# DLRM tower kernel: x goes to SBUF first and is copied from there to PSUM, and ScalarE forms the second layer's sums over d

## The chip, the core and the metric

The kernel runs on one core of one Trainium2 chip. The metric is the device time of one execution in microseconds (us), as a median over runs. A core has TensorE (PE, matrix products), VectorE (DVE), ScalarE (ACT), GpSimd (POOL), SyncE (SP, which only issues transfers here), a buffer SBUF and an accumulator memory PSUM. Every engine works through its own list of instructions in order, and the lists meet at semaphores.

## What is computed

`embeddings` is gathered from 32 tables, (2048, 32 fields, 16 numbers d). Three layers of products of fields follow, each gives 64 rows per sample, and then a small perceptron.

```
x0 = embeddings                       # (b, m, d) = (2048, 32, 16)
xk = x0
for W in (W0, W1, W2):                # (32, h, 64)
    xk = relu(einsum('bmd,bhd,mhk->bkd', x0, xk, W))
    outs.append(sum(xk, axis=2))      # the sum over d
z = concatenate(outs, axis=1)
h = concatenate([z, dense_ctx], axis=1)
h = relu(h @ W_top1 + b_top1); h = relu(h @ W_top2 + b_top2)
y = h @ W_top3
```

All numbers are float32.

## The kernel before

The batch is cut into 32 steps of 64 samples; a step has 1024 columns (64 samples x 16 d). The product of a field with a row of xk is made on the vector engines for 128 (field, row) pairs at a time, a chunk (128 x 1024), and TensorE sums the chunks with the weights: `contract` (L808) issues four matmul records of 512 columns for one chunk. The first layer (`layer0`) takes 5 chunks `p_l0`, the second (`layer1`) and third (`layer2`) take 16 each.

**VectorE** makes 15 of the 16 chunks of each of these two layers (`products`, L706), into a ring of ten chunks, `p_dve`. It multiplies the gathered fields, `spread` (SBUF), with the layer's input x. x lies in PSUM in two forms: `xa`, the plain one, for chunks 0 to 6, and `xb`, with the two halves of 32 rows swapped, for chunks 8 to 15. There is one `xa` and one `xb` for both layers. GpSimd makes chunk 7 (`p_pool`) from a third copy of x, `x_s`, which lies in SBUF, and four of the five first-layer chunks; it also issues the gathers. ScalarE makes the fifth by a square.

**A turn** s of the main loop goes in this order on VectorE: second layer of step s (7 chunks from `xa`, 8 from `xb`), then third layer of step s-1 (again 7 from `xa`, 8 from `xb`). Between them it makes sums over d (`sums`, L728, 128x512 to 128x32): ahead of the first `xb` part those of the second layer of step s-2 (from `out_l[:, 1]`), behind it those of the third layer of step s-2. Sums of the first layer are made by ScalarE from s = 4 on (`sums_0`, L493): one ACTIVATE over 16 columns with an accumulated output for each sample, 32 in a step, in two halves.

**TensorE** in a turn: the 16 chunks of the second layer (accumulator `acc1`, two of them in turns), from s = 4 on with one part of the perceptron behind chunk 5 (`mlp_pair`, parts 0 to 3 in four turns, part 2 twice the size of parts 0 and 1); then third-layer chunks 0 to 3 (`acc2`), the five chunks of the *first* layer of step s+1 (`layer0`, accumulator `acc0`), and third-layer chunks 4 to 15.

**ScalarE** evicts: `relu_a` writes `xa` from the accumulator with 4 ACTIVATEs, `relu_b` writes `xb` with 8, `relu_s` writes `x_s` with 4, and `out_0`, `out_1`, `out_2` write `out_l`. Its list in a turn is hand-written (L636 to L676): `x1_b(s)`, `out_2(s-2)`, `x2_a(s-1)`, half of `sums_0(s)`, `squares(s+1)`, the eviction of the perceptron's part, `x2_b(s-1)`, `x2_s(s-1)`, `out_1(s-1)`, the other half of `sums_0(s)`, in odd turns the moves of finished sums into `z_all` (`move_sums`, L557), then for the next step `x1_a(s+1)`, `x1_s(s+1)`, `out_0(s+1)`. Here x1 is the input of the second layer (from `acc0`), x2 that of the third (from `acc1`); a, b and s stand for `xa`, `xb` and `x_s`. `x1_a(s+1)` waits until VectorE has read the old `xa` and TensorE has finished `layer0(s+1)`; VectorE starts turn s+1 with it. VectorE may write a place of the ring only once TensorE has used the chunk that was there.

Of the kernel before, what the change touches and what calls it, by code (L numbers as in the profile page):

```python
# [7 lines left out]
ACT = mybir.ActivationFunctionType  # L8
# [158 lines left out]
def build_kernel(nc, ids, table, first_row, dense_t, w0_mh, w0_hm, w1, w2, w_top1, b_top1, w_top2,  # L167
                 b_top2, w_top3, scratch, y):
    with ExitStack() as ctx:
# [262 lines left out]
        def _(act):  # L432
# [17 lines left out]
            def relu_s(acc, layer, signal):  # L450
# [21 lines left out]
            def x1_a(s):  # L472

                if s == 1:
                    act.wait_ge(dve_made, POOL_CHUNK)
                if s >= 2:
                    act.wait_ge(dve_made, dve_from(s - 2, 2) + POOL_CHUNK)
                act.wait_ge(l0_used, 2 * (s + 1))
                relu_a(acc0, x1a_ready)

            def x1_s(s):
# [11 lines left out]
            def sums_0(s, part):  # L493
# [9 lines left out]
                if part == 1:  # L503
                    last.then_inc(z_made[0], 1)

            def x1_b(s):

                if s == 1:
                    act.wait_ge(dve_made, CD)
                if s >= 2:  # L510
                    act.wait_ge(dve_made, dve_from(s - 2, 2) + CD)
                relu_b(acc0, x1b_ready)

            def x2_a(s):

                act.wait_ge(dve_used, dve_from(s, 1) + CD)
                if s == 0:
                    act.wait_ge(pool_used, 1)
                if s + 1 < STEPS:
# [3 lines left out]
                relu_a(acc1[s % 2], x2a_ready)  # L523

            def x2_b(s):

                if s + 1 < STEPS:
                    act.wait_ge(dve_made, dve_from(s + 1, 1) + CD)
                else:
                    act.wait_ge(dve_made, dve_from(s - 1, 2) + CD)  # L530
                relu_b(acc1[s % 2], x2b_ready)

            def x2_s(s):

                if s > 0:
                    act.wait_ge(pool_made, pool_from(s - 1, 2) + 1)
                relu_s(acc1[s % 2], 2, x2s_ready)

            def out_1(s):

                if s > 0:
                    act.wait_ge(z_made[1], s)
                nc.scalar.activation(out_l[:, 1, :], acc1[s % 2][:], ACT.Relu).then_inc(out_ready[1], 1)
# [18 lines left out]
            def move_z01(t):  # L562

                act.wait_ge(z_made[0], 2 * (t + 1))
                move_sums(t, 0, 0, 0)
                act.wait_ge(z_made[1], 2 * (t + 1))
                move_sums(t, K, 0, 1)
# [68 lines left out]
            for s in range(STEPS):  # L636
                x1_b(s)
                if s >= 2:
                    out_2(s - 2)
# [54 lines left out]
        def _(dve):  # L694
# [82 lines left out]
            for s in range(STEPS):  # L777
                for c, n in GROUPS_L1:
                    if c == NT:
                        if not sums_by_act(s):  # L780
                            sums(s, 0)
                        if s >= 2:
                            sums(s - 2, 1)
                    if s == 0 and c == L0_OF_1_AFTER[0] + 1:
                        first_layer_half(1, 0, 0, CP)
                    if s == 0 and c == L0_OF_1_AFTER[1] + 1:
                        first_layer_half(1, 1, 0, CP // 2)
                        first_layer_half(1, 1, CP // 2, CP // 2)
                    layer1(s, c, n)
# [17 lines left out]
        def _(pe):  # L807
            def contract(acc, w, prod, start, stop):  # L808
# [234 lines left out]
```

## Time and profile before

| | |
|---|---|
| median of 3 runs | 1167.99 us (1163.64 to 1168.0) |
| profiled execution | 1167.36 us, its span 1165.5 us |
| PE busy | 1106.8 us, 95% of the span |
| DVE busy | 1105.6 us, 95% |
| ACT busy | 904.2 us, 78% |
| POOL busy | 914.4 us, 78% |
| DMA engines, queue q1 | 61.8% |
| granted TensorE clock | 0.9 or more in every slice |

The span is the stretch from the first to the last instruction of the profiled execution; 1.9 us lie around it. A busy share is an average over the whole span: a stretch of the steady part has to be read on its own to see which engine never stops there. "Idle before, releaser" beside an instruction tells how long its engine stood still just before it, and which work ended that.

### The profile page before, as it was taken

How to read it: one execution, taken by the hardware profiler on the slowest of the kernel's cores; microseconds unless marked ns; L12 is line 12 of the kernel's file. 1: busy time of each engine (PE TensorE's matmuls, PEld its weight loads, DVE VectorE, ACT ScalarE, POOL GpSimd, SP SyncE). 2: the span in 40 equal slices, each digit the busy share in tenths (PEclk: the TensorE clock that was granted, in tenths of full speed). 3: DMA queues.
4: the chain of work that ended last, by engine and by line, in shares of the span. 5: the costliest groups of instructions: out<-in, count | busy, mean ns of one | idle time of the engine just before them, and what ended most of it. 6: DMA issues, size and time to landing. Idle time of an engine off the chain costs nothing.

```text
span 1165.5 us, 16445 instructions
## 1 busy us (share of the span) xinstructions
PE 1106.8 (95%) x5342; PEld 384.8 (33%) x5342; DVE 1105.6 (95%) x497; ACT 904.2 (78%) x3106; POOL 914.4 (78%) x639
## 2 busy tenths in 40 slices
PE   0778999999999999999999999999999999999998
PEld 0222223333333333333333333333333333333334
DVE  1589999999999999999999999999999999999994
ACT  0346658788888878887888888888788978889855
POOL 6778788888888888888888888888888888885300
PEclk9999999999999999999999999999999999999999
DMA  6788558866667885766788666678866667876200
GB/s 147 188 217 183 118 130 167 176 145 141 137 141 149 171 175 124 147 147 131 161 175 170 143 144 129 146 154 176 172 131 140 145 142 155 176 163 145 42 1 1
DMA packets 78183, 167.38 MB, mean 144 GB/s; under 512 B 22057, under 2 KB 39746, under 8 KB 78098
## 3 DMA queue, kind: packets, MB, share of 16 engines
q1 hardware_dynamic: 59328, 157.78, 61.8%
q0 software_dynamic: 16384, 4.23, 3.9%
q10 hardware_dynamic: 2386, 4.34, 1.3%
q8 instruction: 42, 0.69, 0.3%
q14 instruction: 43, 0.35, 0.1%
HBM read 157.88 MB, written 8.40 MB: 143 GB/s over the span
## 4 chain that ended last, share of the span: by engine, by line
PE 73%; DVE 13%; issue 6%; ACT 3%; POOL 2%; DMA 2%; ACTq 0%; SPq 0%; DVEq 0%; POOLq 0%
PE acc L811 70%; DVE p_dve L706 12%; PE acc L902 2%; POOL x_rows L378 2%; ACT xb L446 2%; DVE z L733 1%; DMA x_of_steps<-x_rows 1%; PE acc L909 1%; DMA spread<-x_of_steps 1%; ACT x_s L454 0%; ACT xa L437 0%; PE acc L953 0%; DMA x_rows<-in_table,ids_s 0%; POOL p_pool L405 0%; PE acc L945 0%
## 5 line engine op out<-in xcount | busy, mean ns | idle before, releaser
L811 PE MATMUL acc<-p_dve,w_s 128*64 128x512 f32 x3840 | 858.1, 596 | 25.4 <-DVE p_dve L706 24.7
L378 POOL DMA_INDIRECT x_rows<-in_table,ids_s x512 | 493.3, 964 | 146.2 <-issue 131.2
L706 DVE TENSOR_TENSOR p_dve<-spread,xb 128x3072 f32<-128x3072 f32 (+2 forms) x225 | 565.9, 2571 | 2.8 <-issue 2.8
L706 DVE TENSOR_TENSOR p_dve<-spread,xa 128x2048 f32<-128x2048 f32 (+1 forms) x192 | 495.4, 2633 | 7.6 <-ACT xa L437 5.7
L811 PEld LDWEIGHTS acc<-p_dve,w_s 128*64 128x64 f32 x3840 | 272.5, 137 | 575.9 <-issue 476.5
L446 ACT ACTIVATE xb<-acc 32x512 f32<-32x512 f32 x512 | 288.8, 564 | 62.7 <-DVE p_dve L706 56.5
L394 POOL TENSOR_TENSOR p_l<-spread,q_tile 128x2048 f32<-128x2048 f32 x59 | 268.4, 4574 | 8.9 <-DMA q_tile<-x_of_steps 7.9
L437 ACT ACTIVATE xa<-acc 64x512 f32<-64x512 f32 x256 | 145.9, 570 | 100.9 <-PE acc L811 46.7
L405 POOL TENSOR_TENSOR p_pool<-spread,x_s 128x1024 f32<-128x1024 f32 x64 | 152.6, 2384 | 76.1 <-ACT x_s L454 40.7
L501 ACT ACTIVATE out_l<-out_l 128x16 f32<-128x16 f32 x896 | 178.1, 203 | 0.3
L501 ACT ACTIVATION_READ_ACCUMULATOR out_l<-out_l 128x1 f32 x896 | 169.7, 189 | 0.0
L454 ACT ACTIVATE x_s<-acc 64x512 f32<-64x512 f32 x256 | 151.5, 592 | 6.1 <-POOL p_pool L405 2.3
L811 PE MATMUL acc<-p_l,w_s 128*64 128x512 f32 x600 | 133.8, 592 | 0.0
L811 PEld LDWEIGHTS acc<-p_l,w_s 128*64 128x64 f32 x600 | 43.1, 137 | 85.7 <-issue 85.7
L811 PE MATMUL acc<-p_pool,w_s 128*64 128x512 f32 x256 | 65.8, 592 | 0.0
L733 DVE TENSOR_REDUCE z<-out_l 128x32 f32<-128x512 f32 x68 | 45.7, 676 | 5.0 <-ACT out_l L550 5.0
L462 ACT ACTIVATE p_l<-q_tile 128x1024 f32<-128x1024 f32 x30 | 31.5, 1051 | 15.8 <-issue 15.5
L843 PE MATMUL acc<-p_l,w_s 128*64 128x256 f32 x80 | 13.3, 452 | 30.1 <-ACT p_l L470 21.9
L811 PEld LDWEIGHTS acc<-p_pool,w_s 128*64 128x64 f32 x256 | 18.5, 138 | 37.0 <-issue 37.0
L550 ACT ACTIVATE out_l<-acc 128x512 f32<-128x512 f32 x32 | 19.1, 598 | 13.6 <-PE acc L811 13.5
L750 DVE TENSOR_TENSOR p_l<-spread,q_tile 128x1024 f32<-128x1024 f32 (+1 forms) x6 | 9.5, 1589 | 21.0 <-DMA spread<-x_of_steps 21.0
L586 ACT ACTIVATE h<-acc,small 128x256 f32<-128x256 f32 (+1 forms) x54 | 21.2, 448 | 9.9 <-PE acc L902 5.0
(29 smaller groups left out, 206.1 us busy)
## 6 DMA issues: line engine op xcount, KB each, us to landing
spread<-x_of_steps SPq DMA_DIRECT2D x244, 512.0 KB, 16.7
q_tile<-x_of_steps SPq DMA_DIRECT2D x120, 128.0 KB
x_rows<-in_table,ids_s POOLq DMA_INDIRECT x512, 4.1
x_of_steps<-x_rows SPq DMA_DIRECT2D x60, 128.0 KB
spread<-x_of_steps ACTq DMA_DIRECT2D x4, 512.0 KB, 9.9
spread<-x_of_steps SPq DMA_DIRECT2D x6, 256.0 KB, 4.9
w_s<-in_w SPq DMA_DIRECT2D x2, 512.0 KB, 7.0
spread<-x_of_steps SPq DMA_DIRECT2D x8, 128.0 KB, 3.5
```

The lines of the kernel that those rows point to most:

```text
L378: nc.gpsimd.indirect_dma_start(out=x_rows[:, s % 2, i * DIM:(i + 1) * DIM], out_offset=None, in_=table, in_offset=bass.IndirectOffsetOnAxi ...
L394: nc.gpsimd.tensor_tensor(p_l0[:, c:c + 2, :], spread[:, s % 3, c:c + 2, :], q, ALU.mult).then_inc(l0_made, 2)
L405: nc.gpsimd.tensor_tensor(p_pool[:], spread[:, s % 3, POOL_CHUNK, :], x_s[:, layer - 1, :], ALU.mult).then_inc(pool_made, 1)
L437: last = nc.scalar.activation(of_block(xa[to:to + K, :], b), halves(acc[b * K:(b + 1) * K, :]), ACT.Relu)
L446: last = nc.scalar.activation(of_block(xb[q * FIELDS:(q + 1) * FIELDS, :], b), halves(hi if q % 2 == 0 else lo), ACT.Relu)
L454: last = nc.scalar.activation(of_block(x_s[to:to + K, layer - 1, :], b), halves(acc[b * K:(b + 1) * K, :]), ACT.Relu)
L462: nc.scalar.activation(p_l0[:, CP, :], q_tile[:], ACT.Square).then_inc(squares_made, 2)
L501: last = nc.scalar.activation(cols, cols, ACT.Relu, accum_out=z[:, s // 2 % 2, 0, s % 2, i:i + 1])
L706: nc.vector.tensor_tensor(p_dve[:, to:to + n, :], spread[:, s % 3, tile:tile + n, :], over(x[:], n), ALU.mult).then_inc(dve_made, n)
L733: nc.vector.reduce_sum(z[:, s // 2 % 2, n, s % 2, :], out_l[:, n, :].rearrange("p (i d) -> p i d", d=DIM), AX_X).then_inc(z_made[n], 1)
L811: last = nc.tensor.matmul(halves(acc[b * K:(b + 1) * K, :]), w, of_block(prod, b), start=start, stop=stop)
L902: last = nc.tensor.matmul(out[b * K:(b + 1) * K, :], w[:, b * K:(b + 1) * K], x, start=i == 0, stop=i == len(terms) - 1)
```

## The change

Three things change.

1. **x by way of SBUF.** For the second layer from step 2 on and for the third from step 1 on (`copied`), ScalarE no longer reads the accumulator for `xa` and `xb`. It writes `x_s` first, as before with 4 ACTIVATEs, and then `copy_a` writes `xa` with one ACTIVATE of 128x1024 from `x_s`, and `copy_b` writes `xb` with 4 of 32x1024.
2. **Order on ScalarE.** At a turn's end stand `x1_s`, `out_0`, `x1_a` where `x1_a`, `x1_s`, `out_0` stood. `x2_s(s-1)` goes from behind `x2_b(s-1)` to the turn's start, behind `x1_b(s)`. In the tail `x2_s(31)` goes from behind `x2_b(31)` to before `x2_a(31)`.
3. **Sums.** For steps 2 to 29 the second layer's sums leave VectorE (28 TENSOR_REDUCE) and are made by ScalarE, `sums_1(s-2)`, 32 ACTIVATEs in turn s behind `x2_s(s-1)`.

TensorE's waits for a free `acc0` (`x1_is_read`) ask for `x_s` and `out_0` now, and no longer for `xb`.

```
+def copied(s, layer):
+    return s > 1 or layer == 2 and s > 0
+def sums_1_by_act(s):
+    return 2 <= s < STEPS - 2
...
+            def copy_a(layer):
+                return nc.scalar.activation(xa[:], x_s[:, layer - 1, :], ACT.Copy)
+            def copy_b(layer):
+                for q in range(Q):
+                    of = (q + 1) % Q * FIELDS
+                    last = nc.scalar.activation(xb[q * FIELDS:(q + 1) * FIELDS, :],
+                                                x_s[of:of + FIELDS, layer - 1, :], ACT.Copy)
+                return last
...
             def x1_a(s):
...
-                act.wait_ge(l0_used, 2 * (s + 1))
-                relu_a(acc0, x1a_ready)
+                if copied(s, 1):
+                    act.wait_ge(x1s_ready, s + 1)
+                    copy_a(1).then_inc(x1a_ready, 1)
+                else:
+                    act.wait_ge(l0_used, 2 * (s + 1))
+                    relu_a(acc0, x1a_ready)
             def x1_s(s):
+                act.wait_ge(l0_used, 2 * (s + 1))
+                if s > 0:
+                    act.wait_ge(x1b_ready, s)
                 if s > 0:
                     act.wait_ge(pool_made, pool_from(s - 1, 1) + 1)
                 relu_s(acc0, 1, x1s_ready)
...
+            def sums_1(s):
+                act.wait_ge(out_ready[1], s + 1)
+                if s % 2 == 0 and s >= 4:
+                    act.wait_ge(z_moved, s // 2 - 1)
+                for i in range(SB // 2):
+                    cols = out_l[:, 1, i * DIM:(i + 1) * DIM]
+                    last = nc.scalar.activation(cols, cols, ACT.Relu,
+                                                accum_out=z[:, s // 2 % 2, 1, s % 2, i:i + 1])
+                last.then_inc(z1_made_by_act, 1)
...
             def x2_s(s):
+                layer1_is_done(s)
+                if s > 0:
+                    act.wait_ge(x2b_ready, s)
...
             for s in range(STEPS):
                 x1_b(s)
+                if s >= 1 and copied(s - 1, 2):
+                    x2_s(s - 1)
+                if sums_1_by_act(s - 2):
+                    sums_1(s - 2)
                 if s >= 2:
                     out_2(s - 2)
...
                 if s >= 1:
-                    x2_s(s - 1)
+                    if not copied(s - 1, 2):
+                        x2_s(s - 1)
                     out_1(s - 1)
...
-                if s + 1 < STEPS:
+                if s + 1 < STEPS and copied(s + 1, 1):
+                    x1_s(s + 1)
+                    out_0(s + 1)
+                    x1_a(s + 1)
+                elif s + 1 < STEPS:
                     x1_a(s + 1)
                     x1_s(s + 1)
                     out_0(s + 1)
+            x2_s(STEPS - 1)
             x2_a(STEPS - 1)
...
             x2_b(STEPS - 1)
-            x2_s(STEPS - 1)
...
                         if not sums_by_act(s):
                             sums(s, 0)
-                        if s >= 2:
+                        if s >= 2 and not sums_1_by_act(s - 2):
                             sums(s - 2, 1)
...
             def layer0(s, evictions):
...
-                pe.wait_ge(x1b_ready, s)
-                pe.wait_ge(out_ready[0], s)
+                x1_is_read(s - 1)
```

ScalarE's list, first part of a turn of the steady state. `acc` is `acc0` or `acc2`, `acc_0` and `acc_1` are the two `acc1`, `p_l` is `p_l0`. Before:

```order
L446 ACTIVATE xb<-acc 32x2x256 x8
L550 ACTIVATE out_l<-acc 128x512
L437 ACTIVATE xa<-acc_1 64x2x256 x4
L501 ACTIVATE out_l,z<-out_l 128x16 x16
L462 ACTIVATE p_l<-q_tile 128x1024
L586 ACTIVATE h<-acc,small 128x256 x2
L446 ACTIVATE xb<-acc_1 32x2x256 x8
```

After:

```order
L492 ACTIVATE xb<-x_s 32x1024 x4
L480 ACTIVATE x_s<-acc_1 64x2x256 x4
L558 ACTIVATE out_l,z<-out_l 128x16 x32
L626 ACTIVATE out_l<-acc 128x512
L486 ACTIVATE xa<-x_s 128x1024
L546 ACTIVATE out_l,z<-out_l 128x16 x16
L500 ACTIVATE p_l<-q_tile 128x1024
L664 ACTIVATE h<-acc,small 128x256 x2
L492 ACTIVATE xb<-x_s 32x1024 x4
```

The `x_s` of the third layer and 32 accumulating ACTIVATEs now stand between the first `xb` and everything that follows it.

The rest of ScalarE's turn, an odd one with the moves into `z_all`. Before:

```order
L446 ACTIVATE xb<-acc_0 32x2x256 x8
L454 ACTIVATE x_s<-acc_0 64x2x256 x4
L543 ACTIVATE out_l<-acc_0 128x512
L501 ACTIVATE out_l,z<-out_l 128x16 x16
L557 ACTIVATE z_all<-z 64x4x16 x6
L437 ACTIVATE xa<-acc 64x2x256 x4
L454 ACTIVATE x_s<-acc 64x2x256 x4
L491 ACTIVATE out_l<-acc 128x512
```

After:

```order
L492 ACTIVATE xb<-x_s 32x1024 x4
L619 ACTIVATE out_l<-acc_0 128x512
L546 ACTIVATE out_l,z<-out_l 128x16 x16
L633 ACTIVATE z_all<-z 64x4x16 x6
L480 ACTIVATE x_s<-acc 64x2x256 x4
L536 ACTIVATE out_l<-acc 128x512
L486 ACTIVATE xa<-x_s 128x1024
```

`xa` of the next step was the first thing behind the moves and is now the third, behind `x_s` and `out_l`.

VectorE's turn of the steady state. Before:

```order
L706 TENSOR_TENSOR p_dve<-spread,xa 128x3072
L706 TENSOR_TENSOR p_dve<-spread,xa 128x2048 x2
L733 TENSOR_REDUCE z<-out_l 128x32
L706 TENSOR_TENSOR p_dve<-spread,xb 128x3072 x2
L706 TENSOR_TENSOR p_dve<-spread,xb 128x2048
L733 TENSOR_REDUCE z<-out_l 128x32
L706 TENSOR_TENSOR p_dve<-spread,xa 128x2048
```

After:

```order
L793 TENSOR_TENSOR p_dve<-spread,xa 128x3072
L793 TENSOR_TENSOR p_dve<-spread,xa 128x2048 x2
L793 TENSOR_TENSOR p_dve<-spread,xb 128x3072 x2
L793 TENSOR_TENSOR p_dve<-spread,xb 128x2048
L820 TENSOR_REDUCE z<-out_l 128x32
L793 TENSOR_TENSOR p_dve<-spread,xa 128x2048
```

The first of the two reductions of a turn is gone; nothing else moved.

## Rows read from the trace of the kernel before

**Rows 1.** Busy time by engine in the stretch 400 to 800 us

```profile
core 0: us, PE busy (x) PEld busy (x) DVE busy (x) ACT busy (x) POOL busy (x), PEclk, DMA share, GB/s
400.00:800.00 400.00, 398.14 (x1926) 136.82 (x1924) 399.82 (x177) 340.97 (x1220) 341.63 (x236) 1.00 0.71 149
```

**Rows 2.** Timeline of VectorE, turns 17 and 18: start us, us, instruction

```profile
619.98 7.74 DVE L706 TENSOR_TENSOR p_dve<-spread,xa 128x3072 f32<-128x3072 f32 x3
627.64 0.67 DVE L733 TENSOR_REDUCE z<-out_l 128x32 f32<-128x512 f32 x1
628.24 8.80 DVE L706 TENSOR_TENSOR p_dve<-spread,xb 128x3072 f32<-128x3072 f32 x3
636.96 0.67 DVE L733 TENSOR_REDUCE z<-out_l 128x32 f32<-128x512 f32 x1
637.56 7.74 DVE L706 TENSOR_TENSOR p_dve<-spread,xa 128x2048 f32<-128x2048 f32 x3
645.21 8.87 DVE L706 TENSOR_TENSOR p_dve<-spread,xb 128x3072 f32<-128x3072 f32 x4
654.00 7.74 DVE L706 TENSOR_TENSOR p_dve<-spread,xa 128x3072 f32<-128x3072 f32 x3
...
688.17 7.75 DVE L706 TENSOR_TENSOR p_dve<-spread,xa 128x3072 f32<-128x3072 f32 x3
```

**Rows 3.** Chain that ended last: a turn's 148 records, a perceptron part's 32

```profile
392.34 3.45 PE acc L902 x32
395.80 31.76 PE acc L811 x148
```

**Rows 4.** Timeline of TensorE, end of turn 17 and of turn 18

```profile
643.15 1.94 PE L811 MATMUL acc<-p_dve,w_s 128*64 128x512 f32 x8 [0.31 <-DVE p_dve L706]
...
680.13 4.46 PE L811 MATMUL acc<-p_l,w_s 128*64 128x512 f32 x20
684.42 6.18 PE L811 MATMUL acc<-p_dve,w_s 128*64 128x512 f32 x28
```

**Rows 5.** Timeline of ScalarE, without its small sums, turns 17 and 18

```profile
634.53 0.84 ACT L586 ACTIVATE h<-acc,small 128x256 f32<-128x256 f32 x2
...
684.70 2.31 ACT L437 ACTIVATE xa<-acc 64x512 f32<-64x512 f32 x4 [2.79 <-PE acc L811]
```

**Rows 6.** Timeline of ScalarE in turn 17, the small sums and the moves

```profile
644.81 0.20 ACT L501 ACTIVATE out_l<-out_l 128x16 f32<-128x16 f32 x1
...
647.59 0.20 ACT L501 ACTIVATE out_l<-out_l 128x16 f32<-128x16 f32 x1
647.78 1.57 ACT L557 ACTIVATE z_all<-z 64x64 f32<-64x64 f32 x6
649.49 2.31 ACT L437 ACTIVATE xa<-acc 64x512 f32<-64x512 f32 x4
```

**Rows 7.** Groups of ScalarE by shape: busy us, mean ns, idle before

```profile
L446 ACT ACTIVATE xb<-acc 32x512 f32<-32x512 f32 x512 | 288.8, 564 | 62.7 <-DVE p_dve L706 56.5
L454 ACT ACTIVATE x_s<-acc 64x512 f32<-64x512 f32 x256 | 151.5, 592 | 6.1 <-POOL p_pool L405 2.3
...
L462 ACT ACTIVATE p_l<-q_tile 128x1024 f32<-128x1024 f32 x30 | 31.5, 1051 | 15.8 <-issue 15.5
```

**Rows 8.** Timeline of ScalarE, end of turn 1

```profile
105.73 2.31 ACT L437 ACTIVATE xa<-acc 64x512 f32<-64x512 f32 x4 [9.83 <-PE acc L811]
108.07 2.40 ACT L454 ACTIVATE x_s<-acc 64x512 f32<-64x512 f32 x4
```

**Rows 9.** Timeline of VectorE, start of turn 2

```profile
108.14 7.75 DVE L706 TENSOR_TENSOR p_dve<-spread,xa 128x3072 f32<-128x3072 f32 x3 [2.08 <-ACT xa L437]
```

**Rows 10.** Timeline of ScalarE and VectorE in the tail

```profile
1135.70 0.60 ACT L550 ACTIVATE out_l<-acc 128x512 f32<-128x512 f32 x1 [5.11 <-PE acc L811]
...
1141.01 6.68 DVE L706 TENSOR_TENSOR p_dve<-spread,xb 128x3072 f32<-128x3072 f32 x3 [1.15 <-issue]
```

**Rows 11.** Timeline of GpSimd: the same chunk in turns 18 and 19

```profile
656.43 2.38 POOL L405 TENSOR_TENSOR p_pool<-spread,x_s 128x1024 f32<-128x1024 f32 x1 [0.30 <-PE acc L811]
...
691.64 2.39 POOL L405 TENSOR_TENSOR p_pool<-spread,x_s 128x1024 f32<-128x1024 f32 x1 [1.65 <-PE acc L811]
```

More of the change, by code:

```diff
@@ L114, in sums_by_act, with sums_1_until, sums_1_by_dve @@
     return s >= 4
+def copied(s, layer):
+    return s > 1 or layer == 2 and s > 0
+def sums_1_by_act(s):
+    return 2 <= s < STEPS - 2
+def sums_1_until(s):
+    return min(max(0, s - 1), STEPS - 4)
+def sums_1_by_dve(s):
+    return s + 1 - sums_1_until(s)
 def stored(s):
@@ L239, in build_kernel @@
         z_made = [sem(f"z{n}_made") for n in range(3)]
+        z1_made_by_act = sem("z1_made_by_act")
         z_moved = sem("z_moved")
@@ L477, in x1_a, with x1_s @@
                     act.wait_ge(dve_made, dve_from(s - 2, 2) + POOL_CHUNK)
+                if copied(s, 1):
[4 more added lines that the diff above has]
+                    relu_a(acc0, x1a_ready)
+            def x1_s(s):
                 act.wait_ge(l0_used, 2 * (s + 1))
-                relu_a(acc0, x1a_ready)
-            def x1_s(s):
+                if s > 0:
+                    act.wait_ge(x1b_ready, s)
                 if s > 0:
@@ L511, in x1_b, with layer1_is_done @@
                     act.wait_ge(dve_made, dve_from(s - 2, 2) + CD)
-                relu_b(acc0, x1b_ready)
-            def x2_a(s):
+                if copied(s, 1):
+                    copy_b(1).then_inc(x1b_ready, 1)
+                else:
+                    relu_b(acc0, x1b_ready)
+            def layer1_is_done(s):
                 act.wait_ge(dve_used, dve_from(s, 1) + CD)
@@ L518, in x2_a @@
                     act.wait_ge(pool_used, 1)
+            def x2_a(s):
+                if not copied(s, 2):
+                    layer1_is_done(s)
                 if s + 1 < STEPS:
@@ L522, in x2_a @@
                     act.wait_ge(dve_made, dve_from(s - 1, 2) + POOL_CHUNK)
-                relu_a(acc1[s % 2], x2a_ready)
+                if copied(s, 2):
+                    act.wait_ge(x2s_ready, s + 1)
+                    copy_a(2).then_inc(x2a_ready, 1)
+                else:
+                    relu_a(acc1[s % 2], x2a_ready)
             def x2_b(s):
@@ L530, in x2_b @@
                     act.wait_ge(dve_made, dve_from(s - 1, 2) + CD)
-                relu_b(acc1[s % 2], x2b_ready)
+                if copied(s, 2):
+                    copy_b(2).then_inc(x2b_ready, 1)
+                else:
+                    relu_b(acc1[s % 2], x2b_ready)
             def x2_s(s):
+                layer1_is_done(s)
+                if s > 0:
+                    act.wait_ge(x2b_ready, s)
                 if s > 0:
@@ L541, in out_1 @@
                 if s > 0:
-                    act.wait_ge(z_made[1], s)
+                    act.wait_ge(z_made[1], sums_1_by_dve(s - 1))
+                if sums_1_until(s - 1) > 0:
+                    act.wait_ge(z1_made_by_act, sums_1_until(s - 1))
                 nc.scalar.activation(out_l[:, 1, :], acc1[s % 2][:], ACT.Relu).then_inc(out_ready[1], 1)
@@ L565, in move_z01 @@
                 move_sums(t, 0, 0, 0)
-                act.wait_ge(z_made[1], 2 * (t + 1))
+                act.wait_ge(z_made[1], sums_1_by_dve(2 * t + 1))
+                if t > 0:
+                    act.wait_ge(z1_made_by_act, sums_1_until(2 * t + 1))
                 move_sums(t, K, 0, 1)
@@ L813, in contract, with x1_is_read @@
                 return last
+            def x1_is_read(s):
+                pe.wait_ge(x1s_ready, s + 1)
+                pe.wait_ge(out_ready[0], s + 1)
+                if not copied(s, 1):
+                    pe.wait_ge(x1b_ready, s + 1)
             def layer0(s, evictions):
@@ L889, in acc0_is_free @@
             def acc0_is_free(step, evictions):
-                pe.wait_ge(x1b_ready, step + 1)
-                pe.wait_ge(out_ready[0], step + 1)
+                x1_is_read(step)
                 if evictions > 0:
```

## The prediction

> **What bounds the kernel now.** I read first the busy times of a steady stretch, then the timelines of VectorE, TensorE and ScalarE side by side over two turns, then the chain that ended last. In 400 us VectorE is busy for 399.82 [rows 1]: it never stops. TensorE looks as full at 398.14, but a part of that is waiting inside; ScalarE and GpSimd are busy for 341 each. The clock granted is 1.00, the 2.4 GHz level, and the change leaves TensorE as dense as it was.
>
> VectorE's turn [rows 2] lasts 34.02 us (619.98 to 654.00): 7.66 on `xa`, 0.60 for a reduction (start to next start), 8.72 on `xb`, 0.60 for the other, 7.65 and 8.79 for the third layer. The next lasts 34.17: it carries part 2 of the perceptron. Three turns in four are like the first.
>
> TensorE needs 31.76 us for the 148 records of a turn and 3.45 for part 2 [rows 3]; parts 0 and 1 have half its records (1.73 each), part 3 an eighth (0.43). Four turns need 4 x 31.76 + 7.34 = 134.4 us, against 3 x 34.02 + 34.17 = 136.2. So TensorE has 0.46 us of air in a turn. In turn 17 it still waits 0.31 for a VectorE chunk ahead of third-layer chunk 2 [rows 4]; in turn 18, with part 2, it never waits, and its first layer ends at 684.42, 30.42 us into the turn. In turn 17 ScalarE writes `xa` at 649.49 [rows 6], 29.51 into the turn; with the 0.28 us from 684.42 to 684.70 [rows 4, 5] as the delay, the first layer ended there at 29.23.
>
> GpSimd's same chunk is 35.21 us later one turn on, 1.65 of them a wait [rows 11]: it needs 33.56 a turn. Three engines lie within 0.6 us of each other.
>
> **Part 1, the reductions leave VectorE.** 28 turns (4 to 31) lose 0.60 each: the turn's floor on VectorE is 34.02 - 0.60 = 33.42. Alone that is 16.8 us. It can't all come out: four turns would need 133.7 and TensorE needs 134.4.
>
> **Part 2, ScalarE's list.** Unknown is the copy, SBUF to PSUM, 128x1024 or 32x1024. From above: the square of 1024 columns, SBUF to SBUF, takes 1.051, and two of the old 512-column evictions 2 x 0.564 = 1.13. From below: PSUM as the destination is cheaper by 592 - 564 = 28 ns [rows 7], so 1.02. I take 1.02 and 0.01 between instructions, 1.03, since the square differs from it by its destination alone, and keep 0.95 to 1.13. 16 small sums take 16 x 2.78/14 = 3.18 [rows 6], 32 take 6.35; `x_s` 2.42 [rows 8], an `out` 0.62 [rows 10], the perceptron's eviction 0.86 [rows 5], six moves 1.7 (647.78 to 649.49, rows 6), the square 1.07.
>
> An odd turn of ScalarE from VectorE's turn start, with 0.1 to get going: `xb` 4.12, `x_s` 2.42, sums 6.35, `out_2` 0.62, `xa` 1.03, sums 3.18, square 1.07, eviction 0.86, `xb` 4.12, `out_1` 0.5 (the sums behind it start early), sums 3.18, moves 1.7, `x_s` 2.42, `out_0` 0.62, `xa` 1.03, sum 33.3; VectorE starts 0.10 after `xa` (105.73 + 2.31 to 108.14, rows 8, 9). So 33.4 to 33.5 against VectorE's 33.42: just on the edge. I charge 0.07 in turns with part 1, and nothing in odd turns with part 3, whose eviction is a smaller one. The deadlines inside hold: `xa` of the third layer is done at 14.7 (VectorE wants it at 33.42 - 8.79 - 7.65 = 16.98), the second `xb` at 23.9 (wanted at 24.63). The first-layer sums, square and eviction come 3 to 5 us later than before, and what waits for them (TensorE's first layer near 24 us, GpSimd) still comes later. `x_s` for GpSimd's third-layer chunk comes far earlier and GpSimd doesn't wait for it in the steady part, so that is worth nothing there.
>
> At the work's price a page of the Trainium skill says something else. In *ScalarE: Activation LUTs*, under "What ACT_TABLE_LOAD costs", it says that back-to-back ACTIVATEs overlap by about 93 ns. Here four of 592 ns on average last 2.40 us [rows 7, 8], which is no overlap. If copies out of SBUF did overlap, ten copies would save 0.9 us a turn, the edge would be gone, and the total would be lower by 0.4 us, six turns at 0.07.
>
> **Part 3, the order at the turn's end.** Before, `xa` was ready 0.28 + 2.31 us behind the first layer's last matmul. Now it is 0.28 + 2.42 + 0.62 + 1.03 = 4.35, and 0.10 to VectorE: 4.45. This is a loop: VectorE's chunk 3, TensorE's chunks 2 and 3 and first layer, ScalarE's three steps, VectorE's next turn.
> - Ordinary turn: the first layer ends at 29.23 - 0.60 = 28.63, since it hangs on VectorE's chunk 2, which comes 0.60 earlier; up to 0.1 more because TensorE is the later one in the shorter turn. 28.7 + 4.45 = 33.2, under 33.42. Free by 0.2 us.
> - Turn with part 2: TensorE is saturated, the first layer ends at 30.42, plus 0.1. 30.52 + 4.45 = 34.97. Before it was 34.17. The turn is **0.80 longer**, though a reduction has gone; VectorE stands 1.0 to 1.5 us waiting for `xa`. TensorE uses this pause to catch up, so the next turns are ordinary again.
> - Turn 1: ScalarE waits 9.83 us for TensorE and VectorE 2.08 for `xa` [rows 8, 9]. `x1_s` and `out_0` now go ahead: VectorE starts at 105.73 + 4.07 + 0.10 = 109.90, not 108.14: +1.76.
>
> **The sum.**
> - Start: +1.76.
> - Turns 4 to 7, whose perceptron parts are of one tile and small: 4 x -0.60 + 2 x 0.07 = -2.3.
> - Turns 8 to 30: six with part 2 at +0.80, six with part 0 at -0.60, six with part 1 at -0.53, five with part 3 at -0.60: 4.8 - 3.6 - 3.2 - 3.0 = -5.0.
> - Turn 31 and tail: there `xb` waits for `out_2` and so for TensorE, 5.11 us [rows 10], and TensorE is saturated from turn 30 on, whose longer turn lets it begin turn 31 0.7 us less behind: -0.7. The 1.15 us of VectorE's wait [rows 10] shrink by the cheaper `xb`, but TensorE, full to the end, hides that.
>
> Sum -6.2 us: 1167.36 - 6.2 = **1161.2**. The profiled execution is 0.6 below the median of 1167.99.
>
> **Rivals.**
> - *A: ScalarE becomes the bound (slower).* If a copy out of SBUF costs 1.13, ten of them add 1.0 to a ScalarE turn. The 13 odd turns take it in full (+13 us), and in the even ones the second `xb` comes at 24.8, 0.25 behind its date (about +3): 1177. It decides from 1.12 us a copy on. For it: ScalarE's odd turn has no air by my sum. Against it: the square's 1.051. The Trainium skill's *ScalarE: Activation LUTs*, section "Rules for kernel authors", tells to put relu, add and such on VectorE and not on ScalarE, which speaks against this move; the rows agree on the single price (0.60 against 6.35 us). Chance 0.14.
> - *B: the edge costs more than I charge.* 0.04 a copy, or a hidden delay of 0.4 in odd turns: 13 x 0.4 = +5.2, 1166.4, no change that can be told. Chance 0.22.
> - *C: the order at the turn's end costs nothing*, because part 2 turns catch up within their neighbours. Then TensorE's 134.4 for four turns is the bound: 5.75 x (134.4 - 136.2) = -10.4, with -2.4, -0.7 and +1.76: 1155.6. Against it: one `xa` buffer, and every step of the loop is in order on its engine. Chance 0.12.
> - *D: the sums don't leave the bound.* A reduction that had run in VectorE's waits would free nothing. VectorE has none in the steady stretch [rows 1], so I give this 0.02; it would leave +1.8 + 4.8 + 0.6, some 1174.
>
> **How the numbers follow.** The forecast has a chance of 0.50 and a range of its own of 1158 to 1165. A comparison of this kernel can tell about 0.5% (5.8 us) from no change; the forecast lies 6.8 below the median, so about two thirds of its chance fall under "faster" (0.34, with C 0.46) and the rest under "same" (0.16, with B 0.38). Slower: A and D, 0.16. Range 1154 to 1170: forecast, B and C; A lies outside.
>
> **What would show it.** Right: turns of VectorE of 33.4 to 33.5 us, three in four, and every fourth (10, 14, ... 30) at about 35.0 with an idle of 1 to 1.5 us released by `xa`; a copy of 128x1024 at 1.02 us; ScalarE busy for 380 in 400 us; the start of turn 2 1.8 us later. Wrong: odd turns well over 33.5 (copies dear, or a wait of ScalarE I didn't see), VectorE waiting for `xb`, or part 2 turns near 34.2.

## The result and the profile after

| | before | after |
|---|---|---|
| median | 1168.0 us (1163.64 to 1168.6, 9 runs) | 1161.01 us (1159.39 to 1163.38, 9 runs) |
| profiled execution, its span | 1167.36, 1165.5 us | 1163.38, 1161.6 us |
| VectorE busy | 1105.6 us | 1089.6 us |
| ScalarE busy | 904.2 us, 78% | 971.5 us, 84% |

The ratio is 0.9948, with an interval of 0.9938 to 0.9958: 0.5% faster, a small difference, but clear of its interval, and E8 below repeats it. The forecast was 1161.2.

Busy times by engine of the kernel after, in the stretch of [rows 1]:

```profile
400.00:800.00 400.00, 400.00 (x1944) 138.44 (x1942) 396.05 (x166) 374.52 (x1817) 345.15 (x237) 1.00 0.72 152
```

VectorE, which never stopped before, now stands for 4 us of 400, TensorE for none, and ScalarE is at 94% (374.5) where it was at 85%. That TensorE never stands is taken up again under E3: it is nearly the bound now. VectorE's timeline of the kernel after, an ordinary turn (349.11 to 382.54) and one with part 2 (382.54 to 417.45), answers to [rows 2]:

```profile
349.11 7.74 DVE L793 TENSOR_TENSOR p_dve<-spread,xa 128x3072 f32<-128x3072 f32 x3
356.77 8.80 DVE L793 TENSOR_TENSOR p_dve<-spread,xb 128x3072 f32<-128x3072 f32 x3
...
382.54 7.73 DVE L793 TENSOR_TENSOR p_dve<-spread,xa 128x3072 f32<-128x3072 f32 x3
...
414.21 2.29 DVE L793 TENSOR_TENSOR p_dve<-spread,xb 128x2048 f32<-128x2048 f32 x1 [0.36 <-PE acc L898]
417.45 7.75 DVE L793 TENSOR_TENSOR p_dve<-spread,xa 128x3072 f32<-128x3072 f32 x3 [0.95 <-ACT xa L486]
```

The first reduction is gone (7.66 from `xa` to `xb`), the ordinary turn is 33.43 us. The turn with part 2 is 34.91: VectorE waits 0.36 for a place in the ring and 0.95 for `xa`, which is now a copy. TensorE's timeline in that turn answers to [rows 4]:

```profile
393.31 3.62 PE L995 MATMUL acc<-h,wt 128*64 128x256 f32 x32
...
408.78 4.46 PE L898 MATMUL acc<-p_l,w_s 128*64 128x512 f32 x20
413.07 6.18 PE L898 MATMUL acc<-p_dve,w_s 128*64 128x512 f32 x28
```

The first layer ends at 413.07, 30.53 into the turn (30.42 before), and VectorE starts 4.38 us later. ScalarE's groups after answer to [rows 7]:

```profile
L492 ACT ACTIVATE xb<-x_s 32x1024 f32<-32x1024 f32 x244 | 248.7, 1019 | 31.9 <-DVE p_dve L793 28.9
L480 ACT ACTIVATE x_s<-acc 64x512 f32<-64x512 f32 x256 | 151.1, 590 | 65.6 <-PE acc L898 60.4
L486 ACT ACTIVATE xa<-x_s 128x1024 f32<-128x1024 f32 x61 | 62.7, 1028 | 2.9 <-DVE p_dve L793 1.4
```

A copy costs 1.02 to 1.03 us.

**Where the time went**, from the two profiled executions. Start of turns 2, 4 and 31 on VectorE, before (the first is [rows 9]):

```profile
177.38 7.74 DVE L706 TENSOR_TENSOR p_dve<-spread,xa 128x3072 f32<-128x3072 f32 x3
...
1096.90 7.75 DVE L706 TENSOR_TENSOR p_dve<-spread,xa 128x3072 f32<-128x3072 f32 x3
```

and after:

```profile
112.19 7.75 DVE L793 TENSOR_TENSOR p_dve<-spread,xa 128x3072 f32<-128x3072 f32 x3 [4.76 <-ACT xa L486]
...
181.43 7.74 DVE L793 TENSOR_TENSOR p_dve<-spread,xa 128x3072 f32<-128x3072 f32 x3
...
1093.56 7.75 DVE L793 TENSOR_TENSOR p_dve<-spread,xa 128x3072 f32<-128x3072 f32 x3 [0.95 <-ACT xa L486]
```

| stretch | before | after | change | forecast |
|---|---|---|---|---|
| to the start of turn 2 | 108.14 | 112.19 | +4.05 | +1.76 |
| turns 2 and 3 | 69.24 | 69.24 | 0 | 0 |
| turns 4 to 30 | 919.52 | 912.13 | -7.39 | -7.3 |
| turn 31 and tail | 68.60 | 68.04 | -0.56 | -0.7 |

The start needs a closer look. ScalarE's step there, at 105.73 before [rows 8], came at 108.02 after, 2.29 later, and nothing that the change moves has run by then. The other 4.05 - 2.29 = 1.76 is the new order. The 2.29 are traced in the last section. They are most of the reason why the two profiled executions lie only 3.98 us apart and the medians 7.0; the forecast, made from the profiled execution, was 6.2.

### The profile page after: what moved, and what is told of

Same layout as the page of the kernel before. It is cut to its first block, busy times and chain, and to the rows that moved or that the text cites. A ratio compares the mean times of both kernels' runs of the same rounds, so it can differ in the third digit from the quotient of the medians.

```text
span 1161.6 us, 17890 instructions
## 1 busy us (share of the span) xinstructions
PE 1109.1 (95%) x5342; PEld 386.6 (33%) x5342; DVE 1089.6 (94%) x469; ACT 971.5 (84%) x4471; POOL 916.2 (79%) x639
## 4 chain that ended last, share of the span: by engine, by line
PE 84%; ACT 5%; DVE 4%; DMA 2%; issue 2%; POOL 1%; ACTq 1%; SPq 0%; DVEq 0%
PE acc L898 79%; PE acc L995 4%; DVE p_dve L793 4%; POOL x_rows L404 1%; ACT xb L492 1%; DMA spread<-x_of_steps 1%; ACT out_l L558 1%; ACT x_s L480 1%; DMA x_of_steps<-x_rows 1%; PE acc L1002 1%; ACT xb L472 1%; PE acc L1046 0%; DMA x_rows<-in_table,ids_s 0%; ACT xa L463 0%; ACT out_l L546 0%
## 5 line engine op out<-in xcount | busy, mean ns | idle before, releaser
L492 ACT ACTIVATE xb<-x_s 32x1024 f32<-32x1024 f32 x244 | 248.7, 1019 | 31.9 <-DVE p_dve L793 28.9
L558 ACT ACTIVATE out_l<-out_l 128x16 f32<-128x16 f32 x896 | 178.2, 200 | 0.7
L546 ACT ACTIVATE out_l<-out_l 128x16 f32<-128x16 f32 x896 | 177.5, 199 | 0.0
L558 ACT ACTIVATION_READ_ACCUMULATOR out_l<-out_l 128x1 f32 x896 | 167.4, 187 | 0.0
L546 ACT ACTIVATION_READ_ACCUMULATOR out_l<-out_l 128x1 f32 x896 | 167.1, 186 | 0.0
L486 ACT ACTIVATE xa<-x_s 128x1024 f32<-128x1024 f32 x61 | 62.7, 1028 | 2.9 <-DVE p_dve L793 1.4
L820 DVE TENSOR_REDUCE z<-out_l 128x32 f32<-128x512 f32 x40 | 26.8, 676 | 5.5 <-ACT out_l L626 5.5
```

The costliest lines, as they stand in the source:

```text
L486: return nc.scalar.activation(xa[:], x_s[:, layer - 1, :], ACT.Copy)
L492: last = nc.scalar.activation(xb[q * FIELDS:(q + 1) * FIELDS, :], x_s[of:of + FIELDS, layer - 1, :], ACT.Copy)
L546: last = nc.scalar.activation(cols, cols, ACT.Relu, accum_out=z[:, s // 2 % 2, 0, s % 2, i:i + 1])
L558: last = nc.scalar.activation(cols, cols, ACT.Relu, accum_out=z[:, s // 2 % 2, 1, s % 2, i:i + 1])
```

## The experiments

Each is the changed kernel with one edit. "Ratio" is to the kernel before, measured on the same chip in the same batch; the first batch had it at 1166.96, the third at 1167.4.

**E1, the sums alone.**

```
 def copied(s, layer):
-    return s > 1 or layer == 2 and s > 0
+    return False
...
-            x2_s(STEPS - 1)
             x2_a(STEPS - 1)
...
             x2_b(STEPS - 1)
+            x2_s(STEPS - 1)
```

> The changed kernel with xa and xb written from the accumulators again, in the old order; only the sums of the second layer (28 steps) are on ScalarE. Theory (ScalarE has no room for the sums without the copies): its list adds up to 35.1 us in an even turn and 36.8 in an odd one, both over VectorE's 33.42, so 28 turns of 36 us on average: 1168 + 28 x 1.9 = 1221 us, VectorE waiting for xa and xb. Rival (the sums' removal from VectorE is what counts, copies are a side matter): 1168 - 16.8 = 1151.

Measured: 1214.47 us in one run. ScalarE is busy for 392.55 of 400 us, VectorE for 374.92. VectorE's timeline, two turns:

```profile
532.28 7.75 DVE L793 TENSOR_TENSOR p_dve<-spread,xa 128x3072 f32<-128x3072 f32 x3 [1.15 <-issue]
559.02 8.88 DVE L793 TENSOR_TENSOR p_dve<-spread,xb 128x3072 f32<-128x3072 f32 x4 [1.88 <-issue]
567.82 7.74 DVE L793 TENSOR_TENSOR p_dve<-spread,xa 128x3072 f32<-128x3072 f32 x3
594.03 8.88 DVE L793 TENSOR_TENSOR p_dve<-spread,xb 128x3072 f32<-128x3072 f32 x4 [1.50 <-issue]
604.07 7.75 DVE L793 TENSOR_TENSOR p_dve<-spread,xa 128x3072 f32<-128x3072 f32 x3 [1.16 <-issue]
```

532.28 to 604.07 are 71.8 us for two turns, 35.9 each, where the sum of ScalarE's list gave 36.0. VectorE waits for `xb` and `xa` in every turn. So the sums are affordable only because the copies make room, and the rival of the expectation (1151) falls. The total is 6 us under the 1221 expected: such turns are 1.85 us longer than before, but there are 26 of them and not 28. Turn 4 takes 33.73, turn 31 lies in the tail, and turns 4 to 30 together are 47.8 us longer.

**E2, the copies alone.**

```
 def sums_1_by_act(s):
-    return 2 <= s < STEPS - 2
+    return False
 def sums_1_until(s):
-    return min(max(0, s - 1), STEPS - 4)
+    return 0
```

> The changed kernel with all of the second layer's sums back on VectorE; copies and the new order stay. Theory (the order at the turn's end costs in turns with part 2 and in turn 1, and the rest of the copies is hidden): VectorE's ordinary turns 34.02 us as in the kernel before, turns with part 2 at 30.42 + 4.45 = 34.87 instead of 34.17, turn 1 longer by 1.76: 1168 + 6 x 0.7 + 1.8 - 0.7 = 1173. Rival (the order costs nothing): 1168.

Measured: 1173.03 us, ratio 1.0051 (1.0033 to 1.007). VectorE's timeline, an ordinary turn of 34.02 and one with part 2 of 34.80:

```profile
349.38 7.74 DVE L793 TENSOR_TENSOR p_dve<-spread,xa 128x3072 f32<-128x3072 f32 x3
383.40 7.74 DVE L793 TENSOR_TENSOR p_dve<-spread,xa 128x3072 f32<-128x3072 f32 x3
418.20 7.75 DVE L793 TENSOR_TENSOR p_dve<-spread,xa 128x3072 f32<-128x3072 f32 x3 [0.70 <-ACT xa L486]
```

By themselves the copies cost 6 us, in the turns with part 2 and in turn 1. E1 and E2 together: each half of the change makes the kernel slower, and only both make it faster.

**E3, `xa` ahead of `out_0`.**

```
                     x1_s(s + 1)
-                    out_0(s + 1)
                     x1_a(s + 1)
+                    out_0(s + 1)
```

> The changed kernel with out_0 behind x1_a instead of ahead of it (x_s, xa, out). Theory (the delay from the first layer's end to xa sets the turns with part 2): 0.62 us less in the loop, perhaps 0.1 given back because the copy now follows x_s directly; VectorE's turns with part 2 go from 34.91 to 34.4, turn 1 gains 0.5 too: 1161.0 - 3.5 = 1157.5. Rival (TensorE's load alone sets these turns): 34.9 stays, 1161.

Measured: 1159.03 us, ratio 0.9932 (0.9913 to 0.9952). VectorE's timeline, the turn with part 2:

```profile
378.40 7.74 DVE L793 TENSOR_TENSOR p_dve<-spread,xa 128x3072 f32<-128x3072 f32 x3
410.08 2.29 DVE L793 TENSOR_TENSOR p_dve<-spread,xb 128x2048 f32<-128x2048 f32 x1 [0.36 <-PE acc L898]
412.76 7.75 DVE L793 TENSOR_TENSOR p_dve<-spread,xa 128x3072 f32<-128x3072 f32 x3 [0.40 <-ACT xa L486]
```

34.36 us, as expected: 0.55 of the 0.62 moved arrive. So the way from the first layer to `xa` set this turn. But it is the first of the six. The next, turn 14 (513.06 to 547.82), and the four after it take 34.76, only 0.16 less than in the change:

```profile
513.06 7.73 DVE L793 TENSOR_TENSOR p_dve<-spread,xa 128x3072 f32<-128x3072 f32 x3
545.14 2.29 DVE L793 TENSOR_TENSOR p_dve<-spread,xb 128x2048 f32<-128x2048 f32 x1 [0.73 <-PE acc L898]
547.82 7.75 DVE L793 TENSOR_TENSOR p_dve<-spread,xa 128x3072 f32<-128x3072 f32 x3 [0.40 <-ACT xa L486]
```

VectorE waits 0.73 for TensorE there, where it waited 0.36 in turn 10. TensorE's timeline of E3, from the end of the first layer in turn 10 to the same place in turn 14:

```profile
408.93 6.18 PE L898 MATMUL acc<-p_dve,w_s 128*64 128x512 f32 x28
...
424.48 1.02 PE L1002 MATMUL acc<-h,small 128*1 128x256 f32 x4
425.44 2.80 PE L898 MATMUL acc<-p_dve,w_s 128*64 128x512 f32 x12
...
441.80 6.18 PE L898 MATMUL acc<-p_dve,w_s 128*64 128x512 f32 x28
...
543.99 6.17 PE L898 MATMUL acc<-p_dve,w_s 128*64 128x512 f32 x28
```

It has no gap in these four turns and takes 543.99 - 408.93 = 135.06 us, and VectorE's four turns are 3 x 33.43 + 34.76 = 135.06 as well: TensorE's list is what they wait for. The change itself takes 3 x 33.43 + 34.92 = 135.2. So in its long turns from turn 14 on, only 0.16 us is the order's; the rival of the expectation (TensorE's load alone) is wrong for turn 10 and nearly right for the other five. Turns 4 to 30 take 910.25 us in E3 and 912.13 in the change: 1.88 less, of it 0.51 in turns 4 and 5, 0.55 in turn 10 and 0.8 in the other five. The tail gives 0.5 back (68.5 against 68.0), and the start is due to gain 0.5. That is 1.9 us under the change and not the 3.5 expected; measured are 2.0.

**E4, `xa` from the accumulator in turn 1 and in turns with part 2.**

```
+def xa_first(s):
+    return s == 2 or s >= 11 and s % 4 == 3
...
-                if copied(s, 1):
+                if copied(s, 1) and not xa_first(s):
                     act.wait_ge(x1s_ready, s + 1)
                     copy_a(1).then_inc(x1a_ready, 1)
...
-                if s + 1 < STEPS and copied(s + 1, 1):
+                if s + 1 < STEPS and copied(s + 1, 1) and not xa_first(s + 1):
```

(with the waits that this needs: `x1_b` for `x_s`, TensorE's `x1_is_read` for `xa`)

> The changed kernel, but at the end of turn 1 and of the six turns with part 2 xa is written from the accumulator by four ACTIVATEs ahead of x_s, as in the kernel before. Theory: the delay there is 0.28 + 2.31 + 0.10 again; what is late next is the ring, whose free place TensorE gives 3.8 us behind the first layer's end, so these turns take 34.3 (VectorE waits for TensorE, not for xa); turn 1 gains 1.76, the tail gives 0.6 back: 1161.0 - 6 x 0.6 - 1.8 + 0.6 = 1156.2. Rival (TensorE's load alone): 34.9 stays, only turn 1 gains: 1159.2.

Measured: 1161.59 us, ratio 0.995 (0.9932 to 0.9968): no gain over the change, 5.4 over what was expected. VectorE's timeline, the turn with part 2 and the one behind it:

```profile
378.01 7.74 DVE L799 TENSOR_TENSOR p_dve<-spread,xa 128x3072 f32<-128x3072 f32 x3
...
412.30 7.75 DVE L799 TENSOR_TENSOR p_dve<-spread,xa 128x3072 f32<-128x3072 f32 x3 [0.32 <-PE acc L904]
437.75 8.88 DVE L799 TENSOR_TENSOR p_dve<-spread,xb 128x3072 f32<-128x3072 f32 x4 [0.73 <-issue]
446.88 7.75 DVE L799 TENSOR_TENSOR p_dve<-spread,xa 128x3072 f32<-128x3072 f32 x3 [0.25 <-ACT xa L491]
```

The first half of the theory holds: 34.29 us, 34.3 expected, released by TensorE and no longer by `xa`. The second half had forgotten ScalarE. Its `x_s`, `out_0` and then `xb` come 1.9 us behind VectorE's start, in front of an odd turn whose list has no room, and that turn takes 34.58 instead of 33.43: `xb` is late by 0.73, `xa` by 0.25. Of 0.62 won 1.15 are lost again, five times; behind the sixth lies the tail, which is 1.0 longer. This is the direct sight of the edge in ScalarE's odd turns in an undisturbed batch.

**E5, E6, E7: more work for ScalarE, less for TensorE.** E5 and E6 are the change with more work for ScalarE: they write `out_1` twice and three times, each behind a wait for the one before:

```
+                nc.scalar.activation(out_l[:, 1, :], acc1[s % 2][:], ACT.Relu).then_inc(spare_made, 1)
+                act.wait_ge(spare_made, 1 * s + 1)
                 nc.scalar.activation(out_l[:, 1, :], acc1[s % 2][:], ACT.Relu).then_inc(out_ready[1], 1)
```

and E7 leaves out half of part 2's contraction:

```
-                                            for k in range(H1 // P)])
+                                            for k in range(H1 // P // 2)])
```

> The changed kernel with one ACTIVATE more on ScalarE in every turn: out_1 is written twice, the second time behind a wait for the first, 0.6 us and some 0.1 for the wait. Theory (ScalarE's odd turns are at the edge, its even turns have air): in the changed kernel xa is ready 0.27 us ahead of VectorE's need in odd turns with part 1, and in odd turns with part 3 ScalarE has 0.7 us of air (0.4 ahead of the need and 0.3 spent waiting for TensorE). So 0.7 - 0.27 = 0.43 in 7 turns, nothing elsewhere: 1161.0 + 3 = 1164. Rival (ScalarE, 84% busy, has air): 1161. Rival (it is the bound everywhere): 28 x 0.7 = 19.6 more, 1181.

> As the run before with two more ACTIVATEs of out_1, 1.4 us more in every turn. Theory: 1.13 in 7 odd turns with part 1, 0.7 in 6 odd turns with part 3, 0 in even ones: 1161.0 + 12 = 1173. Rival (air): 1161. Rival (bound everywhere): 1200.

> The changed kernel with half of part 2's matmuls left out (two of the four chunks of the contraction over h1), so that part 2 weighs on TensorE like parts 0 and 1, 1.73 us less in six turns and once in the tail. Theory (turns with part 2 are late because TensorE's list is longer there and the longer way to xa no longer hides it): all turns take 33.4, VectorE doesn't wait for xa: 1161.0 - 6 x 1.5 - 1.7 = 1150. Rival (the long turns come from the order or from xa alone, whatever TensorE has to do): 34.9 stays, only the tail gains, 1159.

Measured: 1281.74, 1295.47 and 1273.09 us, all far beyond every expectation, and in this batch the kernel before too took 1203.89 (1203.45 to 1204.57), 37 us more than in the others. ScalarE's timeline in E7, in the middle of `sums_1`, shows the larger part of it:

```profile
438.63 0.22 ACT L558 ACTIVATE out_l<-out_l 128x16 f32<-128x16 f32 x1 [0.34 <-issue]
439.35 0.20 ACT L558 ACTIVATION_READ_ACCUMULATOR out_l<-out_l 128x1 f32 x1 [0.51 <-issue]
440.08 0.22 ACT L558 ACTIVATE out_l<-out_l 128x16 f32<-128x16 f32 x1 [0.32 <-issue]
440.78 0.20 ACT L558 ACTIVATION_READ_ACCUMULATOR out_l<-out_l 128x1 f32 x1 [0.49 <-issue]
```

A small sum with its read of the accumulator, 0.20 us otherwise, takes 1.45 here for some in each run, with pauses of 0.3 to 0.5 us that end on nothing the profile shows. In 400 us they add up to 38.9 us, some 3.6 a turn, and the turns are about as much longer than 33.4 (36.8 from 428.89 to 465.70). ScalarE is the bound there, and what TensorE has to do hardly matters. All of these pauses lie in `sums_1`, a series of 32 sums. The series of 16 (`sums_0`) have none in any of the five traces (in E6 and E11 the moves into `z_all` have some), and turns without `sums_1` are as long as ever (turns 2 and 3 34.62, turn 31 33.44).

The pauses are not the only loss. In E7 turn 2 starts at 136.62 us, in the change at 112.19: ScalarE waits 38.9 us for its first `xa`, where it waited 6.5. No trace of the kernel before was kept in this batch. It has only series of 16 sums, so its 37 us may well be such a late start and not pauses; that is open.

**E11 and E12, the same kernels as E6 and E7 once more.**

> The changed kernel with out_1 written three times, 1.4 us more of ScalarE in every turn, once more: in the batch before, all kernels, the one before too, met pauses in ScalarE's runs of small instructions that none had met till then. Without them, theory (odd turns at the edge, even ones with air): 1.13 in 7 odd turns with part 1, 0.7 in 6 odd turns with part 3, 0 in even ones, 12 us over the changed kernel's 1160 to 1161: 1173. Rival (air in all turns): 1161. Rival (ScalarE the bound everywhere): 1200. Should the pauses come again: about 1295.

> The changed kernel with two of the four chunks of part 2's contraction left out, once more, for the same reason. Without pauses, theory (TensorE's longer list in turns with part 2 makes xa late): all turns 33.4 us, 1161.0 - 6 x 1.5 - 1.7 = 1150. Rival (order or xa alone): 34.9 stays in these turns, 1159. Should the pauses come again: about 1273.

Measured: 1299.45 and 1274.27 us, with the kernel before at 1205.38, on another chip. The waits of E12 in the stretch 400 to 800 us, what waited, for what, us in total, times, longest:

```profile
ACT out_l L558 <- issue: 37.2, 73, 1.2
```

So the pauses came again, with a late start (turn 2 at 139.34 and 124.44), and the two questions (how much air ScalarE has in each kind of turn, and whether TensorE's longer list in turns with part 2 is what makes `xa` late) were not answered by these five runs. The first has E1 and E4; the second has E3's trace, by which TensorE's list accounts for all but 0.16 us of these turns from turn 14 on. No undisturbed run with a shorter list confirms it. What the runs do show is that 1.4 us more on ScalarE costs 22 to 25 us (E6 over E7, E11 over E12), though the two kernels of each pair also differ in part 2.

**E8, E9, E10: the change, E3 again, and E3 with turn 1 as before.** E10's edit is E3's and E4's with `return s == 2`.

> The changed kernel unaltered, beside the two runs that follow, on the same chip. All theories: 0.994 to 0.995 of the kernel before. Its turns from 4 on should be as in the first profile to 0.1 us, and what differs between executions should lie ahead of turn 2: 112.19 us there in the first profile, some 110 expected from the kernel before (108.14 + 1.76).

> x_s, xa, out_0 at the turn's end, once more with more rounds. Theory: six turns of 34.36 instead of 34.91 and 0.5 us in turn 1: 3.8 us under the changed kernel of this batch. Rival: no more than the scatter, 1 us.

> As the run before, and at the end of turn 1 alone xa comes from the accumulator ahead of x_s, where ScalarE has nothing else to do. Theory: VectorE's wait before turn 2 falls to the kernel before's, 1.2 us under the run before and 5 under the changed kernel.

| | median, range | ratio to before |
|---|---|---|
| E8, the change | 1160.04 (1159.57 to 1160.99) | 0.9936 (0.9922 to 0.9949) |
| E9, `xa` ahead of `out_0` | 1158.33 (1155.62 to 1160.08) | 0.9925 (0.9911 to 0.994) |
| E10, and turn 1 | 1157.83 (1156.69 to 1159.72) | 0.9914 (0.99 to 0.9928) |

The change's result repeats. E8's turn 2 starts at 109.84, as expected, but by luck: two deviations of 1.0 us cancel (last section). E10 is faster than the kernel before and than the change; over the change it is 2.2 us at the median, less than the 5 expected, and the two intervals still touch. The expectation had taken E3's first turn with part 2 for all six. In E9 and E10 too it is 34.36 (34.37 and 34.35) in turn 10 and 34.75 to 34.76 in the five others, so the turns give 1.9 us and not 3.3, and E9 should be 1.9 under E8 by the sum above: it is 1.7 under. E10's edit works on VectorE's wait before turn 2, which also depends on the execution:

E9:

```profile
105.75 7.75 DVE L793 TENSOR_TENSOR p_dve<-spread,xa 128x3072 f32<-128x3072 f32 x3 [1.53 <-ACT xa L486]
```

E10:

```profile
109.87 7.75 DVE L799 TENSOR_TENSOR p_dve<-spread,xa 128x3072 f32<-128x3072 f32 x3 [2.08 <-ACT xa L468]
```

E10, meant to wait less, waited longer, since TensorE took 1.70 us more for the 20 records ahead of it, 6.21 against 4.51 (last section). 1.53 + 1.70 - 2.08 leaves 1.15 us for the edit. E3 and E4, which differ by the same step and both had 4.51, say the same: the wait is 1.53 and 0.38. At the medians E10 is 0.5 us under E9, too little to tell.

## Why the prediction was right, point by point

- **What bounds.** VectorE full and ScalarE's sum near 33.3 hold. TensorE's air does not: the prediction took part 3 of the perceptron for an eighth of part 2's time, 0.43 us, because it has an eighth of the records. Its four records, with weights one column wide, take 0.96 us from start to next start (E3's rows, 424.48 to 425.44), and its turn is 1.11 over 31.76 (408.93 to 441.80). Four turns need 135.06 us and not 134.4, and TensorE was 0.3 us a turn behind VectorE, not 0.46. E1 gives ScalarE's sum an independent check, 35.9 measured against 36.0 added up.
- **Part 1.** A reduction is worth 0.60 us: 34.02 to 33.43 in every turn that nothing else delays.
- **The copy**, taken at 1.02 from between 0.95 and 1.13: 1.019 and 1.028. The mix of the square's price and PSUM's cheaper destination was right, and with it rival A's condition (1.12) did not arise.
- **Part 2, the charge of 0.07 us** in odd turns with part 1 was mis-sized: turn 9 takes 33.43, and in turn 13 `xa` is done at 517.38 and VectorE starts at 517.75. ScalarE has 0.27 us of air there and not a lack of 0.07; ACTIVATEs that follow one another out of different memories overlap by up to 0.1 (the copy at 531.43 takes 1.03, the sum behind it starts 0.96 later), which my sum left out in some places. In its stead turn 5 took 33.89: its perceptron part for one tile weighs 1.99 us on TensorE (226.07 to 228.06), more than the 1.73 of a part 1 for two, and I had called it small. The first layer ends 29.50 into that turn (244.41), and with the loop's 4.38 that is 33.88. The two errors nearly cancel, 0.56 too much and 0.46 too little.
- **Part 3, the loop to `xa`.** Forecast 30.52 + 4.45 = 34.97, measured 30.53 + 4.38 = 34.91. VectorE waits 1.31 us in it (forecast 1.0 to 1.5). In turn 10 E3 and E4 move it by what they move in the loop, and E2 shows it without the sums, where TensorE has air: 34.80 against 34.16. In the change itself a second bound lies right under it, TensorE's list at 34.76, and the prediction did not see that. It puts the whole 0.80 down to the order, and 0.60 of it (34.76 against 34.16) would have been there without the new order too. The number is right because the higher of the two bounds was the one summed; that the other lies only 0.16 below is not in the prediction.
- **Rival C** (1155.6) falls as priced. With 135.06 for 134.4 its own sum gives 5.75 x (135.06 - 136.2) - 2.4 - 0.7 + 1.76 = -7.9, so 1159.4, 1.8 under the forecast, and the total alone could hardly tell the two apart. What does is the turns: 34.91 and not 34.76.
- **Turn 1**: +1.76 as forecast, once what came before it is taken off. E2 shows it best, whose 20 records took 6.21 us as in the kernel before: VectorE waits 3.78 for `xa` against 2.08, 1.70 more.
- **The tail**: -0.56 against -0.7. TensorE was the late one to the end: ScalarE's `out_2(30)` waits 5.11 us for it, as in [rows 10].
- **ScalarE's share**: 374.5 in 400 us against 380.
- **Overlapping ACTIVATEs.** By the Trainium skill's *ScalarE: Activation LUTs*, section "What ACT_TABLE_LOAD costs", ten copies would have saved 0.9 us a turn. Four copies of 1.019 each last 4.11 us here (ScalarE's timeline at 517.87), so they don't overlap, and the trace decides against the rule for a run of like copies. The square, 1.04 us long, is followed by the eviction after 0.95 (535.57 to 536.52), so other neighbours do overlap.
- **Rival A** was the nearest danger. Its premise about the copy is wrong, its mechanism is true: in E1, in odd turns of E4 and in the disturbed batches VectorE waits for ScalarE. In those two batches (E5 to E7, E11 and E12) variants of the changed kernel are 5.8 to 7.6% slower than the kernel before (E7 at 1.058, although it does less). The change itself was not run there, so its own ratio in that condition is open, and that it would be above 1 too is argued from the same list on ScalarE, not shown. The forecast had nothing on this condition: the pauses are in no trace that I had.

## What to carry to other kernels

Work moved off the fullest engine is worth no more than the distance to the next one: here VectorE's turns 4 to 30 were freed of 16.2 us, TensorE let 9.3 of them out in E3 and 7.4 in the change, and the order of three instructions cost another 1.8 at the start. So price the next engine's list from its own rows, part by part, and not by counting records: part 3's four took 0.96 us, part 2's thirty-two 3.45. And look at every turn of a kind: the first turn with part 2 promised 3.3 us in all for the repair of the order, and it brought 1.9. Write down each engine's list for one turn with its dates (when each result is wanted), not only its busy sum: a list of 33.3 us in a turn of 33.4 is fine as long as every date is met, and a saving that delays it by 1.9 us once costs more than it brings (E4). Where a result goes through a copy, put nothing between the source and the copy that has no one waiting for it (E3, turn 10 and the start).

## What the runs showed of the hardware that I had not expected

**ScalarE can pause for nothing that the profile shows.** In two of five batches of measurements, on two chips, one of which showed nothing of the kind some minutes earlier, all five profiles have such pauses. Most fall into long series of short instructions: in E7 the first comes behind 15 sums without one (435.29 to 438.63). The series of 16 have none. The Trainium skill, *Runtime: NRT & Kernel Launch*, section "Instruction fetch mechanics", describes each engine fetching its instructions by a queue of its own, a block at a time, hidden because issue is slower than fetch. If the pauses are that fetch, the hiding failed in these batches, 38.9 us in 400. The profile names no releaser. It does show the instruction packets of the queue that grew with ScalarE's list (q14, 43 packets before, 54 after). In 400 to 800 us, in the change and in E7:

```profile
q14 instruction: 21, 0.17, 0.2%
```

```profile
q14 instruction: 20, 0.16, 0.2%
```

The packets are as many and take the same share of the time, and E7 has 81 pauses to its 20 packets. So slower transfers of instructions are not what is seen; what the pauses are stays open.

**Behind a pause of TensorE in turn 1 the clock differs from profile to profile.** TensorE waits there for VectorE, and then 20 records, 4.3 us of work at the full level, follow. The same 20 records in three executions, the change, the kernel before and E9:

```profile
96.50 7.18 PE L898 MATMUL acc<-p_dve,w_s 128*64 128x512 f32 x20 [3.46 <-DVE p_dve L793]
```

```profile
95.12 6.21 PE L811 MATMUL acc<-p_dve,w_s 128*64 128x512 f32 x20 [3.61 <-DVE p_dve L706]
```

```profile
93.28 4.51 PE L898 MATMUL acc<-p_dve,w_s 128*64 128x512 f32 x20 [3.46 <-DVE p_dve L793]
```

The granted clock in the stretch 95 to 100 us is 0.51, 0.66 and 1.00. After waits of the same length the engine goes on at once at 2.4 GHz in one execution and partly at 1.2 GHz in the others, and up to 2.7 us of the kernel's time hang on it. What decides it is not shown. Behind waits of 3.46 us the records took 7.18 and 7.19 in the two profiles of the change, 6.21 in E2, and 4.51 in E1 and E9; E3, the same kernel as E9, had 4.51 behind a wait of 1.76. So it may be chance or hang on the kernel.

It accounts for 1.0 of the 2.29 us by which the start of the profiled execution after was late. The rest was there before that (the records start at 96.50 against 95.12), where VectorE waited 2.50 and 1.57 us for transfers late in turn 0 against 0.33 and 1.32 before. In E8 the records start at 94.15, 1.0 earlier than in the kernel before, and take 7.19, 1.0 longer; that is how its turn 2 comes out at 109.84.
